# Layer-1 attention: the V products and the sum of a head in one run at the head's end, GpSimd adds in one piece, minima by a one-input operation

## The reference, cut to what matters

```python
xn = layer_norm(x, ln_gamma, ln_beta)            # 4 batches, 1024 tokens, 128 wide
q, k, v = heads(xn @ Wq), heads(xn @ Wk), heads(xn @ Wv)   # 16 heads of 64
att = jnp.einsum('bhid,bhjd->bhij', q, k) / 8.0 + alibi_bias(S, 16)[None]
p = jax.nn.softmax(att, axis=-1)
out = jnp.einsum('bhij,bhjd->bhid', p, v)
return merge(out) @ Wo
```

## Time and profile before

| | us |
|---|---|
| median of 3 runs | 2318.41 (2315.52 to 2321.29) |
| the profiled execution | 2305.89 |
| its span, first to last instruction | 2304.0 |

### The profile page before, as it was taken

How to read it: one execution, slowest core, us unless ns; L and a number is a source line. 1 busy time by engine, 2 the same in 40 slices (tenths; PEclk the granted TensorE clock), 3 DMA queues, 4 the chain that set the end, 5 groups by cost and what they waited for, 6 DMA issues and landing times. The chain is left out here.

```text
span 2304.0 us, 40435 instructions
## 1 busy us (share of the span) xinstructions
PE 2197.2 (95%) x10494; PEld 1381.0 (60%) x10531; DVE 1829.4 (79%) x4804; ACT 1234.0 (54%) x1664; POOL 1385.3 (60%) x751
## 2 busy tenths in 40 slices
PE   7989998899999999999999999999999999989995
PEld 4656665456565565656556565655556564449884
DVE  7788886788888888888888888888888887765555
ACT  2232323466666566666656666666666664444442
POOL 2112120578787787878778787887878787643331
PEclk9999999999999999999999999999999999999997
DMA  7050202000000100000100000010000000311114
GB/s 241 22 197 1 85 8 96 21 19 14 16 13 16 35 16 14 13 18 17 34 13 13 21 14 16 13 34 17 14 16 13 20 9 8 148 46 48 46 45 135
DMA packets 90230, 91.25 MB, mean 40 GB/s; under 512 B 22212, under 2 KB 74948, under 8 KB 90120
## 3 DMA queue, kind: packets, MB, share of 16 engines
q1 hardware_dynamic: 85800, 81.35, 11.4%
q0 software_dynamic: 4352, 8.99, 1.2%
HBM read 57.37 MB, written 36.33 MB: 41 GB/s over the span
## 5 line engine op out<-in xcount | busy, mean ns | idle before, releaser
L1624 ACT ACTIVATE big<-P 128x1024 f32<-128x1024 f32 x512 | 512.1, 1020 | 109.2 <-PE P L1993 85.5
L2007 PE MATMUL P<-big,V 128*64 128x512 f32 x2048 | 468.8, 599 | 1.0 <-ACT big L1630 1.0
L649 POOL TENSOR_TENSOR spair<-spair,big 128x1024 f32<-128x1024 f32 x192 | 457.4, 2382 | 15.9 <-DVE hp L810 1.3
L649 POOL TENSOR_TENSOR opair<-opair,big 128x1024 f32<-128x1024 f32 x192 | 457.3, 2382 | 15.0
L1031 DVE CUSTOM_DVE_ANT_0 big<-P,near 128x512 f32<-128x512 f32 x512 | 348.8, 681 | 112.2 <-PE P L1977 108.4
L1977 PE MATMUL P<-kq 96*128 96x512 f32 x1008 | 415.5, 433 | 14.2 <-DVE kq L1015 11.1
L1992 PE MATMUL P<-kq 97*128 97x512 f32 x1024 | 411.4, 402 | 5.7 <-issue 2.8
L1034 DVE TENSOR_REDUCE mhalf<-P 128x1 f32<-128x512 f32 x512 | 349.2, 682 | 79.0 <-PE P L1977 68.5
L1993 PE MATMUL P<-kq 128*128 128x512 f32 x1024 | 408.9, 399 | 0.0
L1977 PEld LDWEIGHTS P<-kq 96*128 96x128 f32 x1008 | 181.8, 190 | 214.3 <-issue 114.0
L2007 PEld LDWEIGHTS P<-big,V 128*64 128x64 f32 x2048 | 135.2, 136 | 265.0 <-issue 262.7
(11 more groups left out here) (316 smaller groups left out, 3663.1 us busy)
## 6 DMA issues: line engine op xcount, KB each, us to landing
slots<-later SPq DMA_DIRECT2D x4, 4224.0 KB, 15.5
kq<-auxrows SPq DMA_DIRECT2D x64, 128.0 KB, 2.3
big<-in_wex SPq DMA_DIRECT2D x8, 768.0 KB, 11.4
xt<-slots SPq DMA_DIRECT2D x76, 66.0 KB, 1.8
near<-in_aux SPq DMA_DIRECT2D x64, 64.0 KB, 1.8
big<-yrows SPq DMA_DIRECT2D x8, 512.0 KB, 7.2
wqk_hi<-wparts SPq DMA_DIRECT2D x62, 64.0 KB, 1.8
wqk_lo<-wparts SPq DMA_DIRECT2D x62, 64.0 KB, 1.9
```

The lines of the kernel that those rows point to most:

```text
L649: pool.tensor_tensor(psum8[s][:, :], psum8[s][:, :], pfull[:, j % RING, :], ALU.add).then_inc(S["p_added"], 1)
L1624: act.activation(pfull[:, j, :], banks(2 * (j % 2)), ACT.Exp, scale=DH1 ** -0.5).then_inc(S["exp_done"], 1)
L2007: mm = pe.matmul(P[64 * i:64 * i + 64, 4, :], V1[:, j, s, :], half(pfull[:, j, :], i), start=(j == 0), stop=(j == T - 1))
```

## The change

TensorE runs all eight V products of a head at its end and then that head's own sum; score blocks, maxima, projections and output products move up or together. VectorE takes `k_low` before `q_low`, both earlier against the biases, and its four reciprocals last in a head. ScalarE copies the sums first thing in the next head, turns both halves of an older head between the first exponentials, and takes `k_high` ahead of exponential 6. GpSimd's scaling stands behind a head's seven adds. `max_both` reduces over an axis of two instead of taking the minimum of two inputs. The core of the diff:

```diff
@@ GpSimd: add_head
                 for j in tiles_:
-                    if behind and j == T - 2:
-                        scaled_out(1 - s, n - 1)
                     k = T * n + j
...
+                if behind:
+                    scaled_out(1 - s, n - 1)
@@ GpSimd: last_pairs
                 add_head(0, 2 * p)
-                add_head(1, 2 * p + 1, True, range(1, T - 2))
-                scaled_out(0, 2 * p)
+                add_head(1, 2 * p + 1)
                 pool.wait_ge(S["h_low_in"], at(16 * b + 16))
...
-                add_head(1, 2 * p + 1, False, range(T - 2, T))
@@ VectorE: max_both
-                    dve.tensor_tensor(mneg[:, b::4], mhalf[rows, 0, :], mhalf[rows, 1, :], ALU.min).then_inc(S["max_both"], 1)
+                    dve.tensor_reduce(mneg[:, b::4], mhalf[rows, :, :].rearrange("p i t -> p t i"), AX.X, ALU.min).then_inc(S["max_both"], 1)
@@ VectorE: head
                 bias(s, n, 1)
-                maxima((1, 1))
+                maxima((1, 1), (2, 0))
+                bias(s, n, 2)
+                maxima((2, 1))
                 if out:
                     add_out(p - 1, 0)
-                maxima((2, 0))
-                bias(s, n, 2)
-                maxima((2, 1))
                 bias(s, n, 3)
                 maxima((3, 0), (3, 1))
                 bias(s, n, 4)
+                maxima((4, 0))
                 if out:
                     add_out(p - 1, 1)
-                maxima((4, 0))
                 bias(s, n, 5)
                 maxima((4, 1), (5, 0))
-                if behind:
-                    invert(o, n - 1, 0)
+                bias(s, n, 6)
+                if ahead == 2:
+                    k_low(s, n + 2, 0)
                 maxima((5, 1), (6, 0))
-                bias(s, n, 6)
+                bias(s, n, 7)
                 maxima((6, 1))
                 if ahead == 2:
                     q_low(s, n + 2, 0)
-                    k_low(s, n + 2, 0)
-                bias(s, n, 7)
-                if behind:
-                    invert(o, n - 1, 1)
                 maxima((7, 0), (7, 1))
                 if ahead:
                     max_both(n + 1)
                     max_rows(n + 1)
...
+                if ahead == 2:
+                    q_low(s, n + 2, 1)
+                    k_low(s, n + 2, 1)
                 if behind:
+                    for c in range(NINV):
+                        invert(o, n - 1, c)
@@ ScalarE: k_high
+                if not isinstance(n, int) or n > 1:
+                    act.wait_ge(S["st_mm"], T * (n - 2) + (i + 1) * TPH + ST_AT)
+                act.wait_ge(S["qk_mm"], 2 * n + i + 1)
@@ ScalarE: head
+                if behind == 2:
+                    sums(o, n - 1)
                 exps(n, 0)
+                if behind == 2:
+                    turned_out(s, n - 2, p - 1, 0)
                 exps(n, 1)
+                if behind == 2:
+                    turned_out(s, n - 2, p - 1, 1)
                 if s == 0:
                     values(p, 0)
-                if behind == 2:
-                    turned_out(s, n - 2, p - 1, 1)
                 exps(n, 2)
+                if behind:
+                    outputs(o, n - 1)
...
                 exps(n, 5)
-                if behind:
-                    outputs(o, n - 1)
+                if ahead == 2:
+                    k_high(s, n + 2, 0)
+                exps(n, 6)
                 if ahead == 2:
                     q_high(s, n + 2, 0)
...
@@ TensorE: project_v, project_qk
+                        pe.wait_ge(S["s_copied"], 2 * p)
...
-                    if not isinstance(n, int) or n > 2:
-                        pe.wait_ge(S["s_copied"], n - 2)
-                    elif n == 2:
-                        pe.wait_ge(S["v_in"], 2)
+                        pe.wait_ge(S["v_in"], n)
+                    elif isinstance(n, int) and n == 3:
+                        pe.wait_ge(S["s_copied"], 1)
+                    else:
+                        pe.wait_ge(S["x_added"], n - 3 + X_AT)
@@ TensorE: head
                 maxima((2, 0))
                 scores(s, n, 2)
                 maxima((2, 1))
+                if out:
+                    pe.wait_ge(S["s_copied"], n)
+                    out_proj(p - 1, 0)
                 scores(s, n, 3)
                 maxima((3, 0))
-                if out:
-                    out_proj(p - 1, 1)
                 if s == 0:
                     project_v(p, 1)
                 maxima((3, 1))
                 scores(s, n, 4)
                 maxima((4, 0))
+                if out:
+                    out_proj(p - 1, 1)
...
                 scores(s, n, 5)
                 maxima((4, 1))
-                if behind:
...
-                    sum_head(o, n - 1)
+                if s == 0 and ahead == 2:
+                    project_qk(s, n + 2, 0)
                 maxima((5, 0))
+                if s == 1 and ahead == 2:
+                    project_qk(s, n + 2, 0)
                 scores(s, n, 6)
-                maxima((5, 1))
-                if ahead == 2:
-                    project_qk(s, n + 2, 0)
-                maxima((6, 0))
+                maxima((5, 1), (6, 0))
                 scores(s, n, 7)
-                maxima((6, 1))
-                weigh(s, n, p, 0)
-                weigh(s, n, p, 1)
-                weigh(s, n, p, 2)
-                maxima((7, 0), (7, 1))
+                maxima((6, 1), (7, 0), (7, 1))
                 if ahead == 2:
                     project_qk(s, n + 2, 1)
-                weigh(s, n, p, 3)
...
+                for j in range(T):
+                    weigh(s, n, p, j)
+                if ahead == 2:
+                    pe.wait_ge(S["q_lo"], 2 * n + 6)
+                    pe.wait_ge(S["k_lo"], 2 * n + 6)
+                else:
+                    pe.wait_ge(S["v_in"], 2 * p + 2)
+                sum_head(s, n)
```

More of the change, by code:

```diff
@@ L741, in _ @@
             add_head(0, HEADS - 2)
-            add_head(1, HEADS - 1, True, range(1, 4))
+            add_head(1, HEADS - 1, False, range(1, 4))
             inverse_root("d0")
@@ L1650, in head @@
                 exps(n, 4)
-                if behind:
+                if behind == 1:
                     sums(o, n - 1)
                 exps(n, 5)
-                if behind:
-                    outputs(o, n - 1)
+                if ahead == 2:
+                    k_high(s, n + 2, 0)
+                exps(n, 6)
                 if ahead == 2:
                     q_high(s, n + 2, 0)
-                    k_high(s, n + 2, 0)
-                exps(n, 6)
-                if ahead:
-                    k_again(o, n + 1)
                 exps(n, 7)
@@ L1665, in head @@
                     k_high(s, n + 2, 1)
+                if ahead:
+                    k_again(o, n + 1)
                 if ahead == 2:
                     q_again(s, n + 2)
-                if behind:
-                    turned_out(o, n - 1, p - 1 if s == 0 else p, 0)
             act.sem_inc(S["exp_done"], EXP_AT)
@@ L1766, in route_exp @@
                 act.activation(rexp[:, :, 0:E1], rlog[:, :, 0:E1], ACT.Exp).then_inc(S["rd_exp"], 1)
+            sums(0, HEADS - 2)
             exps(HEADS - 1, 0)
+            turned_out(1, HEADS - 3, ALL_PAIRS - 2, 0)
             exps(HEADS - 1, 1)
@@ L1772, in _ @@
                 exps(HEADS - 1, j)
-            sums(0, HEADS - 2)
+            outputs(0, HEADS - 2)
             exps(HEADS - 1, 5)
-            outputs(0, HEADS - 2)
             exps(HEADS - 1, 6)
@@ L2043, in head @@
                     project_v(p, 0)
-                if out:
-                    if ahead:
-                        pe.wait_ge(S["q_lo"], 2 * n + 4)
-                        pe.wait_ge(S["k_lo"], 2 * n + 4)
-                    else:
-                        pe.wait_ge(S["s_copied"], n - 1)
-                    out_proj(p - 1, 0)
                 maxima((2, 0))
@@ L2062, in head @@
                 maxima((4, 0))
+                if out:
+                    out_proj(p - 1, 1)
+                if behind == 1:
+                    pe.wait_ge(S["q_lo"], 2 * n + 4)
+                    pe.wait_ge(S["k_lo"], 2 * n + 4)
+                    sum_head(o, n - 1)
                 scores(s, n, 5)
                 maxima((4, 1))
-                if behind:
-                    if s == 0:
-                        pe.wait_ge(S["v_in"], 2 * p + 2)
-                    elif out:
-                        pe.wait_ge(S["x_added"], 2 * p + X_AT)
-                    else:
-                        pe.wait_ge(S["q_lo"], 2 * n + 4)
-                        pe.wait_ge(S["k_lo"], 2 * n + 4)
-                    sum_head(o, n - 1)
+                if s == 0 and ahead == 2:
+                    project_qk(s, n + 2, 0)
                 maxima((5, 0))
+                if s == 1 and ahead == 2:
+                    project_qk(s, n + 2, 0)
                 scores(s, n, 6)
-                maxima((5, 1))
-                if ahead == 2:
-                    project_qk(s, n + 2, 0)
```

(19 more changed lines are left out.)

5 lines of the change are left out of this document (removed).

## The result

The changed kernel takes 2373.16 us (median of 4 runs, 2369.33 to 2376.30), beside 2317.36 for the kernel before (4 runs): slower, ratio 1.0235 with a 95% interval of 1.0217 to 1.0253. The forecast was 2369, range 2325 to 2415.

What follows compares the result with a forecast made beforehand. TensorE was taken to bound the kernel (95% busy), VectorE a close second (79%). +67 us for 61 heads less 16 for minima, +51 on 2305.89, gave 2357; 12.5 for the median's distance made 2369 us, range 2325 to 2415.

Steps and rivals of the forecast that it cites:

- One run instead of three: TensorE's V products and sum in one run per head: two runs' borders less, 2 x 0.35 = 0.70 us saved.
- The end of a head: From product (5,0) to the second Q/K projection, TensorE waits for VectorE: 1.8 us even, 1.5 odd, mean 1.65.
- Score block 2: In odd heads block 2 comes earlier and waits for the first exponential: about 0.3 us, 0.15 per head.
- Per head +1.10: Sum per head of -0.70, +1.65 and +0.15 us; over heads 1 to 61, +67 us.
- Minima, -16 us: VectorE's two-input minima, held by GpSimd's adds at three batch boundaries, become one-input: some 11 + 5 = 16 us saved.
- At no cost: Reciprocals at VectorE's head end, covered by V products (12.5 against 13.8 us); GpSimd's scaling, ScalarE's copies and added waits also free.
- The last two heads: At the end, the sum of the head before is gone and scaling follows the adds: under 2 us either way.
- GpSimd as the limit: Rival, chance 0.12: GpSimd's seven adds, needed by the sum, set the head at 23.3 us; 2296 us in all.
- Held one-input minima: Rival, chance 0.03: each of VectorE's four minima waits for a GpSimd add, 8 us per head, 2860 us.
- borders that stay: Rival, chance 0.03: a head's first V product costs, not the border, so nothing is saved: 43 us more, 2412.
- The falling clock: Rival, chance 0.03: granted clock falls behind the new waits in each head, 61 x 1.7 = 104 us more, 2473.

Runs made afterwards that it cites:

- the split kernels: Changed kernel with two j of V products put back between maxima (6,1) and (7,0): 2310.99 us; with three VectorE order changes too: 2290.95 us.
- the doubled (6,0): Changed kernel with maximum (6,0) reduced twice on VectorE, ahead of the second projection, one result going to an unused column: 2477.96 us.

## Why the prediction was right

- **One run instead of three, -0.70 per head.** Right. In the changed kernel the run from 1025.94 to score block 0 at 1034.72 takes 8.78 us: nine times 0.855, three plain steps of 0.232, and 0.385 for the borders, against 0.355 forecast, so 0.67 are saved. The single product put into it shows the border by itself.
- **The end of a head, +1.65.** Right: 1.64 in the even head (1.8 forecast), 1.5 in the odd one (1.5). VectorE was through with q_low at 1025.24, 4.75 after product (5,0), against 4.90; it started 0.44 behind the product and not 0.58. Work put in front of the projection lengthens the head by most of its own length (0.54 for 0.60, 0.15 for 0.20), and by more where the clock falls; work behind it costs nothing, and TensorE work put beside the queue removes the waits.
- **Score block 2, 0.15 per head.** Right: 0.26 in the odd head's row, 0.32 by the experiment, in every second head.
- **Per head +1.10.** Measured (24.47 + 24.70)/2 - 23.42 = +1.16, over 61 heads 71 us instead of 67. The terms as measured, -0.67 + 1.57 + 0.13, make 1.03. What is missing is a term that the forecast did not have, the longer step behind a wait: 0.1 us once in an even head and twice in an odd one, 0.15 in the mean, which makes 1.18. The waits, forecast 0.08 too long, made up for part of it by luck.
- **Minima, -16 us.** Right in mechanism: -15.3 by itself in the kernel before. In size partly luck: the sum of 7 waits was placed at three boundaries with three falls of the clock, and stood at more places with two falls there; and in the changed kernel's order the edit alone is worth 9.5 us of the heads; the rest of the 18.5 us below went with the new order.
- **At no cost.** Right. VectorE's reciprocals end 12.0 us behind (5,0) (12.5 forecast, cover 13.8), with 2.56 us left; four of them take 3.39 us and not 4 x 0.94, since 0.94 is a duration and the step from one to the next is shorter. The adds end at 22.25 us into the head; the 22.2 of the rival's working was exact, but the head is longer than that.
- **The last two heads, under 2 us.** From head 62's first maximum to the first product of the shared expert it was 48.6 us, before 47.1: +1.5. It is not shown to be the change's: the kernel before with one-input minima has 48.6 there too, and the kernels with the changed order have 46.4 to 48.6.
- **The rivals.** GpSimd as the limit: not even in the split kernels, whose heads reach 23.2 to 23.7 with the sum on time; the 23.3 worked out for it was too careful, since bias 0 sets the first exponential and can be moved. Held one-input minima and borders that stay: refuted. The falling clock: one head in 61, so the range need not have held it; but it was nearer than its chance of 0.03 says, since 0.15 us more of waits brought it to 18 heads.

Sum: 71 for the heads' length less 18.5 for the long heads of before make 52.5 us (forecast 51); the medians differ by 55.8, and the 3.3 us between the two are not placed.

## What to carry to other kernels

Before work is gathered into one run, ask what ran beside it: the V products looked like an interruption of the maxima and were the time in which VectorE caught up. Count both engines' steps between two points where they must meet; idle time of the slower one elsewhere in the loop does not help, since two PSUM banks let it work ahead by two reductions only. Where both a border and a wait can be had, keep just enough of the other engine's work in the gap (here two j of eight; other numbers were not tried), and test each part of a change alone: the part worth keeping here, one line, was hidden under a loss over four times its size.

## What the runs showed of the hardware

- Several waits in a row, with brackets of 0.70 and 0.30 us in the rows of the doubled (6,0), were enough to bring the granted clock down to 0.57 over 4 us behind them, which cost about 1.65 us; no single long idle stretch was needed, unlike the 2.08 us of the earlier trace rows. The same waits did it in some heads and not in others (42 of 61), so a little more of waits can cost far more than its length: 0.15 us more per head cost 36 us instead of 9.
- A two-input minimum of 8 columns waits for the end of a running add of 1024 columns, and the next one gets through in the gap between two back-to-back adds, 0.08 us in the rows above, so four of them cost two adds and not four (3.22 us).
- A plain product behind a wait of TensorE takes 0.33 to 0.34 us to the next one instead of 0.232.
